# ScalarE's exponential and lower branch of an attention block, each cut into two instructions over VectorE's two column parts

## The reference

```
h = x @ kernel
scores = leaky_relu(concat(h[src], h[dst]) @ kernel_attention, 0.2)
e = exp(clip(scores, -2, 2))
alpha = e / (segment_sum(e, src) + 1e-7)
out = segment_sum(h[dst] * alpha, src)
x = layernorm(x + out)
```

## Time and profile before

| | us |
|---|---|
| median of 3 runs | 2108.68 |
| lowest, highest | 2106.03, 2110.29 |
| the profiled execution | 2116.28 |
| its span in the trace | 2114.4 |
| PE, DVE, ACT, POOL busy | 1711.5, 1595.5, 1301.9, 1166.0 |

### The profile page before, as it was taken

How to read it: one execution, slowest core, us unless ns; L and a number is a source line. 1 busy time by engine, 2 the same in 40 slices (tenths; PEclk the granted TensorE clock), 3 DMA queues, 4 the chain that set the end, 5 groups by cost and what they waited for, 6 DMA issues and landing times.

```text
span 2114.4 us, 52410 instructions
## 1 busy us (share of the span) xinstructions
PE 1711.5 (81%) x15382; PEld 1488.1 (70%) x15382; DVE 1595.5 (75%) x3352; ACT 1301.9 (62%) x2361; POOL 1166.0 (55%) x1198
## 2 busy tenths in 40 slices
PE   5788887887778768888888889888888888888887
PEld 3567776777676557777777778777777777777774
DVE  6999998888876657777767767767776777776677
ACT  6146777787886646666656655656565665665564
POOL 4045667676760265555555566555556555556640
PEclk9999999999997889999999999999999999999998
DMA  4034556676672443333333333333333333333331
GB/s 101 20 73 94 102 104 119 120 121 118 120 116 53 138 119 109 109 107 107 107 101 109 109 105 110 106 105 106 107 108 109 109 109 105 105 107 108 108 86 31
DMA packets 141999, 216.65 MB, mean 102 GB/s; under 512 B 27997, under 2 KB 96849, under 8 KB 141914
## 3 DMA queue, kind: packets, MB, share of 16 engines
q0 software_dynamic: 49632, 123.31, 22.6%
q1 hardware_dynamic: 89128, 90.73, 18.4%
q10 hardware_dynamic: 3154, 1.60, 0.4%
HBM read 166.19 MB, written 10.28 MB: 83 GB/s over the span
## 4 chain that ended last, share of the span: by engine, by line
PE 49%; issue 10%; another core or an unknown queue 2%; ACT 2%; DVE 1%; ACTq 0%; DMA 0%; SPq 0%; DVEq 0%
PE ps L1357 11%; PE ps L1363 10%; PE ps L1358 9%; PE ps L1337 8%; PE psA L1375 4%; PE ps L1332 4%; PE ps L1342 2%; ACT h_hi L1409 1%; PE ps L1093 0%; ACT h L1413 0%; DVE x L1174 0%; ACT h L1417 0%; PE ps L1101 0%; DVE stats L1183 0%
## 5 line engine op out<-in xcount | busy, mean ns | idle before, releaser
L1310 POOL DMA_INDIRECT ga<-table_a,idx x784 | 777.7, 992 | 540.0 <-PE ps L1363 184.4
L1413 ACT ACTIVATE h<-ps 128x512 bf16<-128x512 f32 x392 | 233.9, 597 | 488.5 <-PE ps L1363 295.8
L1357 PE MATMUL ps<-wm_hi,h_hi 128*128 128x256 f32 x1568 | 428.1, 303 | 99.0 <-issue 71.3
L1485 DVE SCALAR_TENSOR_TENSOR rest<-ps,h 128x512 f32<-128x512 f32 x392 | 269.3, 691 | 241.3 <-ACT h L1413 203.7
L1358 PE MATMUL ps<-wm_lo,h_hi 128*128 128x256 f32 x1568 | 404.1, 288 | 39.9 <-issue 39.8
L658 POOL DMA_INDIRECT head_n<-scr_eye,row_at x250 | 303.3, 1213 | 228.3 <-issue 223.2
L1357 PEld LDWEIGHTS ps<-wm_hi,h_hi 128*128 128x128 f32 x1568 | 302.3, 193 | 158.6 <-issue 107.2
L1358 PEld LDWEIGHTS ps<-wm_lo,h_hi 128*128 128x128 f32 x1568 | 303.0, 193 | 63.8 <-issue 63.5
L1363 PE MATMUL ps<-wm_hi,h_lo 128*128 128x256 f32 x1568 | 276.9, 288 | 54.9 <-issue 52.1
L1490 DVE TENSOR_TENSOR h<-rest,h 128x512 bf16<-128x512 f32 x392 | 269.3, 687 | 46.9 <-issue 26.7
L1479 DVE SCALAR_TENSOR_TENSOR h_lo<-ps,h_hi 128x512 fp32r<-128x512 f32 x392 | 262.8, 690 | 24.0 <-ACT h_hi L1409 13.5
(11 more groups left out here) (212 smaller groups left out, 2496.4 us busy)
## 6 DMA issues: line engine op xcount, KB each, us to landing
dstb<-scr_dst SPq DMA_DIRECT2D x196, 126.0 KB
cnt<-stage SPq DMA_DIRECT2D x125, 195.3 KB
cnt<-stage SPq DMA_DIRECT2D x125, 109.9 KB
ga<-table_a,idx POOLq DMA_INDIRECT x784
bw<-table_b SPq DMA_DIRECT2D x196, 63.0 KB
table_b<-cnt SPq DMA_DIRECT2D x12, 336.0 KB
head_n<-scr_eye,row_at POOLq DMA_INDIRECT x250
table_a<-upper SPq DMA_DIRECT2D x12, 224.0 KB
```

Source lines behind the costliest of these rows:

```text
L1310: pool.indirect_dma_start(ga[:, u, k, :], None, table_a, bass.IndirectOffsetOnAxis(ap=idx[:, u, k:k + 1], axis=0)).then_inc(gathered[u][k] ...
L1357: pe.matmul(ps2[q][:, t % 2, :], hi, w_hi[:, k, :], start=False, stop=True, skip_group_check=True)
L1485: dve.scalar_tensor_tensor(rest1[:, u % 2, 2 * q:2 * q + 2, :], ps2[q][:, :, :], 0.0, h2[0][:, u % 2, 2 * q:2 * q + 2, :], ALU.max, ALU.su ...
```

## The change

Each of the two ScalarE instructions over 3125 columns becomes two, over VectorE's column parts. Exp part 0 comes after window 0 and part 1 after window 1; low part 0 comes after window 2 and part 1 after window 3. Each exp part waits only for its own leaky part, each leaky part for its own low part, and each weigh part for its own exp part. Nothing else changes.

```
-EXP_AT = 0
-LOW_AT = 1
+EXP_AT = (0, 1)
+LOW_AT = (2, 3)
...
-            def exp(b):
-                slot = pr[(b + 1) % PR]
-                act.wait_ge(leaky_ready, (b + 1) * 2)
+            def exp(b, part):
+                slot = pr[(b + 1) % PR][:, slice(*PROB_CUTS[part])]
+                act.wait_ge(leaky_ready, b * 2 + part + 1)
                 act.activation(slot, slot, ACT.Exp, bias=centre[:, 0:1]).then_inc(exp_ready, 1)
...
-                    if u == EXP_AT and v >= 0:
-                        exp(v)
-                    if u == LOW_AT:
+                    if u in EXP_AT and v >= 0:
+                        exp(v, EXP_AT.index(u))
+                    if u in LOW_AT:
...
-                        act.activation(slot, s1r[0:BLK, :], ACT.Relu, bias=T.s2_low[:, bass.ds(b, 1)], scale=SLOPE).then_inc(low_ready, 1)
+                        cols = slice(*PROB_CUTS[LOW_AT.index(u)])
+                        act.activation(pr[(v + 2) % PR][:, cols], s1r[0:BLK, cols], ACT.Relu, bias=T.s2_low[:, bass.ds(b, 1)], scale=SLOPE).then_inc(low_ready, 1)
             blocks(act, body)
-            exp(NBLK - 1)
+            for part in range(2):
+                exp(NBLK - 1, part)
...
-                if part == 0:
-                    dve.wait_ge(low_ready, t * BPT + v + 2)
+                dve.wait_ge(low_ready, (t * BPT + v + 1) * 2 + part + 1)
...
-                    dve.wait_ge(exp_ready, t * BPT + v + 1)
+                dve.wait_ge(exp_ready, (t * BPT + v) * 2 + part + 1)
```

More of the change, by code:

```diff
@@ L817, in body @@
             def body(t, v):
-                slot = pr[(v + 2) % PR]
                 b = t * BPT + v + 1
```

## The result

The change makes the kernel slower: 2133.36 us median (2130.33 to 2133.75, 4 runs) against 2107.66 us of the kernel before in the same runs. The ratio is 1.0118, with a 95% interval of 1.01 to 1.0135. The forecast was 2137.7 us, 29.0 over the median then known; the time rose by 25.7.

The account below looks back on a forecast made before the run. VectorE, the fullest engine in the attention stage, sets a body's length by its work plus its waits. 9.1, 15.1 and 8.3 make 32.5 us, less 3.0, so 29 us: 2137.7 us, range 2107 to 2151.

Parts of the forecast that it names:

- A body's start is leaky part 0 plus a constant: Attention stage: VectorE waits for nothing from leaky part 0 to the next weigh, so later leaky delays the next body.
- The waits at weigh: VectorE ahead of weigh: 14 waits, 37.0 us; exp's cut starts weigh 1.0 us earlier where exp ends the wait.
- The lengths: Cut ScalarE instructions: 1875 columns take 1.85 us, 1250 take 1.33 us, together 0.29 us longer than the one.
- Term 1: Eight late even bodies, 8 to 22: leaky part 0 starts 1.14 us later in each, 9.1 us together.
- Term 2: Nine odd bodies, 7 to 23: low part 0 waits behind TensorE's window 2; 15.1 us, less 3.0 for bodies 15 and 23.
- Term 3: Bodies 0 to 6: later leaky part 0 costs 8.3 us, of which body 0 gives most, 2.5 us.
- The constants: Time from leaky part 0 to the next body's first stage copy: 9.6 us in body 10, 12.5 in body 11, unchanged.
- rival D: TensorE's clock falls ahead of the next body's first window in eight even bodies: +6 us, 2144 us; chance 0.12.
- Rival B: Weigh's gain is real, leaky isn't late, if low part 0 ends by 7.2 us: -11 us, 2098 us; chance 0.12.
- Rival C: Something taken for hidden, such as GpSimd or DMA, paces bodies; later leaky costs nothing: 2106 to 2113 us; chance 0.08.

Follow-up runs that it names:

- e3: Kernel before with only low cut in two, after windows 2 and 3, exp whole after window 0: 2121.1 us against 2094.84, ratio 1.0117.
- e5: Changed kernel with both leaky parts moved on VectorE behind window 4 and weigh part 1: 2112.8 us, ratio 0.9984 to the kernel before.
- r_after: Changed kernel timed again, unaltered, on another chip beside the kernel before: 2143.79 us against 2116.58, ratio 1.013.
- e1_order: Changed kernel with its four parts reordered, exp 0, low 0, exp 1, low 1 after windows 0 to 3: 2081.26 us against 2094.84 before, ratio 0.993.
- e6: Changed kernel with exp part 0 at the previous body's end, low parts after windows 0 and 2, exp part 1 after 1: 0.9963 of the kernel before.
- e7: As e1_order, but low part 1 after window 2, right behind exp part 1: ratio 0.9948 to the kernel before, 10.8 us under it.
- e8: e1_order with a fourth stage buffer (STAGES = 4): 1784.62 us against 1801.41 for the kernel before, ratio 0.9907.
- r_order: The kernel of e1_order timed again on another chip: 1784.59 us against 1801.41 for the kernel before, ratio 0.9905.

## Why the prediction was right

*A body's start is leaky part 0 plus a constant.* Shown by e3, e5 and the trace. Summed over all bodies, the step from a body's first copy to leaky part 0 grew by 26.4 us in the changed kernel, and the step from there to the next body shrank by 1.2 us. The first copy of all came 0.7 us earlier. 26.4 - 1.2 - 0.7 is 24.5, the 24.5 us of the last copy. In r_after, the same kernel on another chip, the first step is 25.5 us longer than in that trace of before.

*The waits at weigh.* The prediction counted 14 waits with 37.0 us there, which are those that name the DMA; with the five that name exp they are 19 with 46.4 us. Of its sum nothing hangs on that, as it rests on leaky part 0 alone.

*The lengths.* 1.85 us for 1875 columns and 1.33 us for 1250, as forecast from two rows. By line, from 300 to 668 us after (busy us, mean ns):

```profile
L803 ACT ACTIVATE xw<-xw,centre 125x1875 f32<-125x1875 f32 x10 | 18.5, 1846 | 0.0
...
L803 ACT ACTIVATE xw<-xw,centre 125x1250 f32<-125x1250 f32 x9 | 12.0, 1329 | 0.0
```

*Term 1, late even bodies.* Forecast 8 x 1.14 = 9.1 us, measured 10.2. Seven of them have leaky part 0 at 10.1, as worked out. Body 12 has it at 11.3, behind a late stage copy that wasn't in the sum (last section); in r_after, the same kernel, it has it at 10.15, so these 1.2 us belong to one execution.

*Term 2, odd bodies from 7 to 23.* Forecast 15.1 less 3.0, or 12.1 us; measured 7.3. **This is the term that was too large.** The mechanism stands: low part 0 waits for the stage copy of TensorE's window 2. But I took the end of window 2 where it was before, at 7.3 to 9.6 after the first copy; after the change it is 7.2 in all eight bodies from 9 to 23, and leaky part 0 is at 10.4 in each. I had allowed for that in bodies 15 and 23 alone. Its cause stays open. It isn't that window 1 is copied sooner: in e3 that copy is at 4.8 as before, and window 2 ends at 7.2 in the same eight bodies. The DMA engines were busy 0.67 of the late stretch before and 0.57 after, which would suit gathered rows that come sooner, but no run tried that by itself.

*Term 3, bodies 0 to 6.* Forecast 8.3 us, measured 8.9.

*The constants.* Forecast unchanged, measured -1.2 us in all: -1.65 in bodies 0 to 6, +1.2 in late even ones, -0.7 in odd ones. In body 11 it went from 12.5 to 11.5. TensorE's granted clock (third figure from the end) goes with it. Before, in the stretch that ends with the first copy of body 12:

```profile
400.20:403.90 3.70, 3.16 (x14) 2.64 (x15) 3.70 (x13) 0.04 (x1) 2.77 (x4) 0.65 0.68 123
```

and after, in the same place:

```profile
412.20:416.30 4.10, 2.14 (x14) 1.94 (x15) 4.10 (x13) 1.23 (x3) 2.99 (x4) 1.00 0.60 114
```

The same 14 matmuls are busy for 3.16 us at 0.65, part of it at the lower level of 1.2 GHz, and for 2.14 us at 1.00, the upper level of 2.4 GHz. In the other odd bodies of the two traces from 7 on it is the same: the step is 11.5 us where the clock of the last 3.7 us ahead of the next first copy was 1.00, 12.5 where it was 0.54 to 0.66, and in between where the clock was. But that the change moved the fall isn't shown. The step is 12.5 in bodies 9, 11, 15 and 21 before, in 9, 13 and 19 after, and in 11 and 17 of r_after, the same kernel again. In both executions of the changed kernel TensorE stood idle from 411.1 to 413.6 us, ahead of the stretch of body 11; behind it the clock was 1.00 in one and 0.54 in the other.

So the mechanism of rival D is there, a clock that falls next to the path, but only one late even body of eight clearly pays for it: body 22 in this trace, with 10.5 instead of 9.6 at 0.73 (body 14 in r_after, the same figures). D's 6 us didn't come.

*Rival B* needed low part 0 to end by 7.2. In the change it ends at 10.1. In e1_order, where it ends at 6.9, leaky part 0 starts at 7.2 with no wait and the kernel gains 13.6 us, about the 11 of B. That bears out B's condition; it does so by another order of the parts, so it isn't a test of B's sum. The change lay on the other side of that point. *Rival C* is out: nothing took up the loss.

*The difference that is left.* The terms of the forecast add up to 29.5 us, which it rounded to 29; the medians rose by 25.7. Term 2 gave 4.8 us less than forecast and the constants 1.2 less, terms 1 and 3 gave 1.7 more. With the 0.7 us at the start, 29.5 becomes the 24.5 of the two traces; the medians differ by 1.2 us more than that, which lies within the spread of the runs. That the number came so close owes something to errors of either sign.

## What to carry to other kernels

Before a producer is cut to serve a consumer's first part sooner, write the start of each consumer in its engine's own order, and look for the one from which on that engine has no more idle time; it alone sets the pace. Here part 0 of low came 1.0 us shorter but 2.2 us later, and the same four instructions in an order that follows VectorE's (exp 0, low 0, exp 1, low 1) gain 14 us where the order by kind (exp 0, exp 1, low 0, low 1) loses 26 or 27. A part that can't come sooner does no harm if the consumer does other work first (e5). And once one wait is out, the next in line takes much of the gain (e6, e7).

## What the runs showed of the hardware that wasn't expected

Now and then a stage copy starts late, and the timeline shows nothing that holds it. In body 12 of the changed kernel:

```profile
421.19 0.69 ACT L827 ACTIVATE stage<-psC 126x626 f32<-126x626 f32 x1 [1.10 <-PE psC L725]
```

By the rows TensorE ended that window's last matmul at 418.41, 2.2 after the first copy, and this is 4.9; ScalarE itself stood idle for 1.10 us. The copy has one more thing to wait for, the DMA of the window three before, which used the same buffer. That is what e8's expectation took it for. The trace doesn't bear it out: that DMA was issued at 406.7 and 407.4, its packets end at 411.0, and its last landing is at 412.4. What stands right ahead of the copy, by 0.02 us, is the event of the semaphore by which TensorE reports the window, at 421.17. In e1_order's body 8 it is the same with 2.54 us:

```profile
325.06 0.69 ACT L827 ACTIVATE stage<-psC 126x626 f32<-126x626 f32 x1 [2.54 <-remote]
```

There the matmul ends at 321.07, the DMA has landed at 316.3, and TensorE's semaphore moves at 325.04. The kernel before has such copies too (1.07 us in body 20), so they didn't come with the change. What keeps the semaphore 2.8 and 4.0 us behind the matmul's end isn't shown; ends of matmuls are modelled in this profile. For a reader the lesson is that a cause found by ruling out the others has to be looked up as well, here by the landing of its DMA.

The message stage runs at very different speeds on different chips, with one and the same kernel. Stretch 800 to 1200 us of e1_order (busy PE, PEld, DVE, ACT, POOL, then clock, DMA share, GB/s):

```profile
800.00:1200.00 400.00, 337.85 (x3559) 297.60 (x3559) 289.54 (x543) 243.83 (x484) 234.31 (x242) 0.99 0.38 108
```

and of r_order, the same kernel on another chip:

```profile
800.00:1200.00 400.00, 400.00 (x4596) 370.73 (x4595) 362.00 (x701) 314.60 (x623) 305.14 (x312) 1.00 0.52 140
```

From the last stage copy to the end it took 1449.9 us on the one and 1157.3 us on the other, while the attention stage ended at 629.6 and 623.3. On the faster chip the profile shows TensorE busy all 400 us, and the DMAs move 140 GB/s against 108. What differs between the chips wasn't found. It is over ten times the effect that was studied here, so kernels from different chips can't be compared but by their ratio to the kernel before on the same one.
